# An AdaLN feed-forward kernel with low-rank adapters and a mixture of experts: which queue carries which load, and in which order

## The chip, the cores and the metric

The kernel runs on one core of a Trainium2 chip. The time is device microseconds (us) of one execution. The kernel before takes 495.52 us, the median of three runs (491.48 to 496.64).

Engines are named as in the profile: PE does matrix products (PEld its weight loads), DVE and ACT do elementwise work, POOL is GpSimd, SP only issues transfers. A transfer can be issued from SP (queue q1), ACT (q10) or POOL (q0).

## What is computed

All data is float32. `x` is 8 batches of 512 tokens by 2048 features. Each batch picks, by its token `itok`, one of 8 adapters of rank 16, and the adapter's output `c` goes through a linear layer with a routed low-rank update:

```
c    = (x @ B_sel.T) @ A_sel.T                       # rank 16: conditioning's B and A
base = c @ base_w.T + base_b                         # 2048 x 2048
res  = c @ ffn_A.T                                   # 64 wide
p    = softmax(c @ router_w.T)                       # 16 experts; the top two, renormalized
out  = x + base + 0.5 * sum_e comb[e] * (res @ ffn_B[e].T)
```

Since `c` has rank 16, the kernel never forms it. It multiplies the eight selected `A` (8 x 16 = 128 columns) with `base_w` once into a small matrix `G`, folds `ffn_A` and the router into tables in the same way, and then handles each batch's tokens with short contractions.

## The kernel before

**Two parts.** The first part prepares the weights: it loads and transposes `base_w`, forms `G`, and transposes the experts `ffn_B`. It runs from the start to about 157 us. The main loop then takes the 8 batches, each in 16 tiles of 128 tokens by 512 outputs.

**The first part's backbone** is 128 products, n = 0 to 127 (`w_product`, line 792). `base_w` comes in 8 pieces of 2.10 MB, 16 products to a piece. A piece is loaded as four transfers of 512 KB, one for each quadrant q of 32 partitions, in packets of 2 KB (`load_w`, line 272). There are four buffers, so piece n waits for the transposes of piece n - 4 (`s_wt`). DVE transposes 32 x 32 blocks for each product (`w_transpose`), at most 8 products ahead of PE. Product 0 also needs the selected columns of conditioning's `A` (`take_a`, after DVE's seventh transpose), 1.05 MB that lie in HBM in runs of 128 bytes: 32 transfers of 32 KB, 8192 packets in all (`load_cond_a`).

**Between the products** PE's order is fixed by hand. `E_AT` maps a product number to an expert group: ahead of products 12, 20, 30, 38, 50, 58, 66, 74, 97, 104, 111 and 119, PE transposes ("flips") the groups 0 to 11. Groups 12 to 15 follow at tiles 0, 1, 2 and 5 of the main loop (`E_LATE`). A group is 0.52 MB over all 128 partitions, in packets of 1 KB. It goes into one of four slots (`E_SLOT`); its load waits until the slot's last group is flipped (`s_ef`), and is issued by ACT in `copy_experts`, behind that flip. PE waits in `expert_flips` for the group's load. The products 80 to 95 have batch 0's `x` transposed beside them (`X_AT`), from `xquad0`, 4.19 MB loaded by `load_x0`.

**Who issues what.** SP: quadrants 0 and 1 (partitions 0 to 63) of all `base_w` pieces and of `xquad0`, half of conditioning's `A`, the bias, then the stores of `G`, its reloads (`load_gm`), and loads of `x` for the main loop. POOL: quadrants 2 and 3 (partitions 64 to 127) of the `base_w` pieces and of `xquad0`, between its own computing. ACT: the other half of conditioning's `A`, all of `B`, `ffn_A` and the router (`load_small`, 0.66 MB), and all experts. Each queue executes its instructions in program order: a wait holds everything behind it on that engine.

Of the kernel before, what the change touches and what calls it, by code (L numbers as in the profile page):

```python
# [35 lines left out]
P = 128  # L36
# [5 lines left out]
def adaln_ffn(nc, x, itok, cond_A, cond_B, base_w, base_b, ffn_A, ffn_B, router_w, out):  # L42
    NB, T, D = x.shape
    NAD, _, RK = cond_A.shape
# [37 lines left out]
    with ExitStack() as ctx:  # L82
# [130 lines left out]
        E_AT = {12: 0, 20: 1, 30: 2, 38: 3, 50: 4, 58: 5, 66: 6, 74: 7, 97: 8, 104: 9, 111: 10, 119: 11}  # L213
        E_LATE = {0: 12, 1: 13, 2: 14, 5: 15}
        E_SLOT = (0, 1, 2, 0, 1, 2, 0, 1, 2, 0, 1, 3, 0, 1, 3, 0)
        E_FIRST, E_FRESH, EIN_AT = 3, 11, 98
        GHI_AT, GLO_AT = 34, 38
        XRES_AT, XQ_AT = 104, 120
        EB = 0
# [10 lines left out]

            return [k for k in range(g + 1, GROUPS) if E_SLOT[k] == E_SLOT[g]][:1]

        def load_experts(eng, g):

            c, q, i = e_where(g)
            if e_users(g):
                eng.wait_ge(s_ef, e_users(g)[-1] + 1)
            elif g == E_FRESH:
                eng.wait_ge(s_bxq, KD)
            eng.dma_start(e_in[E_SLOT[g]], bexp_v[c, q, i]).then_inc(s_ein[E_SLOT[g]], 16)  # L240

        def load_small(eng, qs):

# [28 lines left out]
        def load_w(eng, n, qs):  # L272

            need(eng, s_wt, (n - WB + 1) * KD)
            for q in qs:
                eng.dma_start(w_in[n % WB][q * SQ:(q + 1) * SQ], w_q[n, q]).then_inc(s_load[q // 2][n % WB], 16)
# [10 lines left out]
        def load_cond_a(eng, ns):  # L287

            for n in ns:
                for q in range(NQ):  # L290
                    eng.dma_start(conda_q[q * SQ:(q + 1) * SQ, n, :, :], condA_q[n, q]).then_inc(s_conda, 16)  # L291
# [8 lines left out]
        @block.sync  # L300
        def _(sp):
            def store_g(g):

                sp.wait_ge(s_glo, g + 1)
                sp.dma_start(g_dram[:, :, g * BANK:(g + 1) * BANK].rearrange("l p o -> p l o"),
                             g_out[g]).then_inc(s_gst, 16)

            def load_gm(b, c):

                for rep in range(2):  # L310
                    for l in range(2):
                        row = (2 * rep + l) * RK
                        sp.dma_start(f32(gm_r[row:row + RK, c * BANK:(c + 1) * BANK]),
                                     g_dram[l, b * RK:(b + 1) * RK, c * BANK:(c + 1) * BANK]).then_inc(s_gm[c], 16)

            load_w(sp, 0, (0, 1))
            for row in (64, 96):
                sp.dma_start(bias_n[row:row + 1, :], base_b.rearrange("(a o) -> a o", a=1)).then_inc(s_bias, 16)
            load_cond_a(sp, range(0, NAD // 2))
            for n in range(1, 6):  # L320
                load_w(sp, n, (0, 1))
            load_x0(sp, (0, 1))
            store_g(0)
            load_w(sp, 6, (0, 1))
            load_w(sp, 7, (0, 1))
            store_g(1)
            sp.wait_ge(s_gst, 32)
            for c in range(2):
                load_gm(0, c)
            sp.wait_ge(s_wt, 6 * KD)  # L330
            for c in range(0, OC, 2):
                load_xres(sp, 0, c)
            store_g(2)
            sp.wait_ge(s_wt, 7 * KD)
            load_xquad(sp, 1, 0, (0, 1))
            sp.wait_ge(s_gst, 48)
            load_gm(0, 2)
            sp.wait_ge(s_wt, 8 * KD)
            load_xquad(sp, 1, 1, (0, 1))
            store_g(3)  # L340
            sp.wait_ge(s_gst, 64)
            load_gm(0, 3)

            def step(b, f):
                for c in range(OC):
                    if f is None and c == OC - 1:
                        for t in range(NT):
                            sp.wait_ge(s_out, b.n * MT + NT * c + t + 1)
                            sp.dma_start(out_v[b.n, :, t, c * BANK:(c + 1) * BANK],
                                         xres[:, t, c * BANK:(c + 1) * BANK]).then_inc(s_store[c], 16)  # L350
                        continue
                    if f is not None and c < 2 and not is_last(f):
                        xquad_free(sp, f, c)
                        load_xquad(sp, f.n + 1, c, range(0, NQ // 2))
                    sp.wait_ge(s_out, b.n * MT + NT * (c + 1))
                    sp.dma_start(out_v[b.n, :, :, c * BANK:(c + 1) * BANK],
                                 xres[:, :, c * BANK:(c + 1) * BANK]).then_inc(s_store[c], 16)
                    if f is None:
                        continue
                    load_gm(f.n, c)  # L360
                    if c > 0:
                        reload(b, f, c - 1)
                if f is not None:
                    reload(b, f, OC - 1)

            def reload(b, f, c):

                sp.wait_ge(s_store[c], b.n * 16 + 16)
                load_xres(sp, f.n, c)

            batches(step)
            for c in range(OC):
                sp.wait_ge(s_store[c], 16 * NB + (16 * (NT - 1) if c == OC - 1 else 0))
# [1 line left out]

        @block.gpsimd
        def _(pool):
            load_w(pool, 0, (2, 3))
            pool.memset(ffna_q[:, R // SQ, :], 0.0).then_inc(s_const, 1)
            pool.wait_ge(s_const, 1)  # L380
            pool.memset(ident[:, :], 0.0).then_inc(s_idn, 1)
# [1 line left out]
            pool.affine_select(out=ident[:, :], in_=ident[:, :], compare_op=ALU.not_equal, fill=1.0, base=0,  # L383
                               pattern=[[-1, P]], channel_multiplier=1).then_inc(s_idn, 1)

            load_w(pool, 1, (2, 3))
            fills = [(f32(gm_r[64:P, :]), 0.0), (table[:, :, :], 0.0), (f32(sbx_r[64:P, :, :]), 1.0)]
            pool.wait_ge(s_idn, 2)
            for n, (where, value) in enumerate(fills):
# [4 lines left out]
            pool.wait_ge(s_iota, 1)  # L394
            pool.wait_ge(s_tok, 16)
            ids = [adapter(pool, b) for b in range(NB)]
            load_w(pool, 2, (2, 3))
            load_w(pool, 3, (2, 3))

            pool.wait_ge(s_bias, 32)  # L400
            for n, row in enumerate((64, 96)):
# [2 lines left out]
            pool.tensor_tensor(gm_r[96:97, :], bias_n[96:97, :], f32(gm_r[96:97, :]), ALU.subtract)\  # L404
                .then_inc(s_biaslo, 1)

            load_w(pool, 4, (2, 3))
            pool.wait_ge(s_bT, KC)
            pool.wait_ge(s_biaslo, 1)
            for b in range(NB):  # L410
                pool.tensor_copy(bT[:, :, b // 2, b % 2 * RK:(b % 2 + 1) * RK],
                                 bT_all[:, :, bass.ds(ids[b], 1), :].rearrange("p j n k -> p j (n k)"))\
                    .then_inc(s_bsel, 1)
            load_w(pool, 5, (2, 3))
            load_x0(pool, (2, 3))
            for n in range(6, PIECES):
                load_w(pool, n, (2, 3))

            def front(f):

# [26 lines left out]
        def _(act):  # L447
# [2 lines left out]

            act.dma_start(tok[:, :], itok.rearrange("(a b) -> a b", a=1)).then_inc(s_tok, 16)
            load_cond_a(act, range(NAD // 2, NAD))
            load_cond_b(act, range(NQ))
            act.wait_ge(s_const, 1)
            load_experts(act, 0)
            load_small(act, range(NQ))
            for g in range(1, E_FIRST):
                load_experts(act, g)
            act.wait_ge(s_idn, 2)
            act.activation(mx[:, 0:1], ident[:, 0:1], ACT.Copy)  # L460

            def copy_experts(g):

                act.wait_ge(s_ef, g + 1)
                for k in e_next(g):
                    load_experts(act, k)
                for at, there, count in ((0, s_a, NB), (0, s_bT, KC), (1, s_fat, 2), (1, s_sm, 1),
                                         (2, s_xe, KD)):
                    if g == PER_C * at:
                        act.wait_ge(there, count)  # L470
                c, q, i = e_where(g)
                src = ps[:, EB:EB + 2, :].rearrange("p b o -> p (b o)")\
                    .rearrange("p (a h m) -> p a m h", a=EG, h=2)
                dst = bexpT[q * R:(q + 1) * R, c, i * EG:(i + 1) * EG, :].rearrange("r a (m h l) -> r l a m h", h=2, l=2)
                for l in range(2):
                    ins = copy(dst[:, l], src[l * R:(l + 1) * R])
                ins.then_inc(s_ec, 1)
# [49 lines left out]

            first = Batch(0)
            for n in range(NW):
                if n == EIN_AT:  # L530
                    load_experts(act, E_FRESH)
                if n == XRES_AT:
                    act.wait_ge(s_wt, 6 * KD)
                    for c in range(1, OC, 2):
                        load_xres(act, 0, c)
                if n == XQ_AT:
                    act.wait_ge(s_wt, 7 * KD)
                    load_xquad(act, 1, 0, (2, 3))
                if n == NW - 1:
                    act.wait_ge(s_wt, NW)  # L540
                    load_xquad(act, 1, 1, (2, 3))
                if n >= GHI_AT and n % (2 * KD) == GHI_AT % (2 * KD):
                    g_hi(n // (2 * KD) - 1)
                if n in E_AT:
                    copy_experts(E_AT[n])
                if n in SLOT_AT:
                    if SLOT_AT[n] in UP_AT:
                        act.wait_ge(s_gst, 16 * (W_GROUPS - 1))
                    slot(first, SLOT_AT[n], False)
# [235 lines left out]
        def _(pe):  # L785
# [16 lines left out]

            def expert_flips(g):

                pe.wait_ge(s_ein[E_SLOT[g]], 16 * (len(e_users(g)) + 1))
                need(pe, s_ec, g)
                for k in range(2 * EG):
                    ins = flip(EB + k // 4, k % 4 * P, e_in[E_SLOT[g]][:, k // 2, k % 2 * P:(k % 2 + 1) * P])
                ins.then_inc(s_ef, 1)
# [134 lines left out]
```

## Time and profile before

| | |
|---|---|
| median of three runs | 495.52 us (491.48 to 496.64) |
| the profiled execution | 494.57 us, of which the span is 492.4 us |
| PE busy | 415.0 us (84%) |
| DVE busy | 292.1 us (59%) |
| ACT busy, POOL busy | 109.1 us (22%), 58.7 us (12%) |
| moved by DMA | 135.30 MB, mean 275 GB/s |
| DMA queues: share of 16 engines' span | q1 (SP) 60.4%, q10 (ACT) 20.0%, q0 (POOL) 8.2% |
| chain that ended last | PE 64%, DVE 12%, DMA 11%, ACTq 7% |

The span runs from the first to the last instruction of the profiled execution; 2.2 us lie around it. Queue names with a q at the end (ACTq) are an engine's issuing of transfers. The chain is the work that ended last, followed back step by step to what released it.

### The profile page before, as it was taken

Reading aid. Unit: us, or ns where it says so; the run is one execution under the profiler, and the core shown is the slowest. Engines: PE = TensorE matmul, PEld = TensorE weight load, DVE = VectorE, ACT = ScalarE, POOL = GpSimd, SP = SyncE. Lnnn points to the kernel's source line nnn. Section 1 sums busy time; section 2 is a strip of 40 time slices with the busy share of each in tenths; the row PEclk is TensorE's granted clock in tenths of the full one; section 3 lists DMA queues with packets and bytes.
Section 4 is the critical chain, followed back from the end, with each engine's and each line's share of the span. In section 5 each row is a group of like instructions: output and inputs, shape, how many; then the busy total and the mean of one; then the engine's idle time right before and its main releaser. Section 6 shows DMA issues by size and latency. Waiting matters only on the chain.

```text
span 492.4 us, 6151 instructions
## 1 busy us (share of the span) xinstructions
PE 415.0 (84%) x2240; PEld 276.2 (56%) x2240; DVE 292.1 (59%) x699; ACT 109.1 (22%) x166; POOL 58.7 (12%) x72
## 2 busy tenths in 40 slices
PE   0009199577898899999999999999999999999997
PEld 0008178463574556656655665665566566556675
DVE  0116266448682665675766667566776755776453
ACT  0001150330362623202311320230121023013210
POOL 5800210100011001200300120120012012001200
PEclk9999699979998999999999999999999999999999
DMA  8999999996799589988978998897999899835854
GB/s 187 216 251 243 278 273 291 298 281 192 254 279 303 168 269 325 324 285 288 375 274 289 342 322 283 294 366 269 293 354 323 274 289 366 300 121 177 309 194 172
DMA packets 95059, 135.30 MB, mean 275 GB/s; under 512 B 13812, under 2 KB 50676, under 8 KB 95028
## 3 DMA queue, kind: packets, MB, share of 16 engines
q1 hardware_dynamic: 62516, 97.03, 60.4%
q10 hardware_dynamic: 29666, 27.40, 20.0%
q0 software_dynamic: 2848, 10.49, 8.2%
q8 instruction: 18, 0.29, 0.3%
q14 instruction: 11, 0.09, 0.1%
HBM read 99.24 MB, written 35.65 MB: 274 GB/s over the span
## 4 chain that ended last, share of the span: by engine, by line
PE 64%; DVE 12%; DMA 11%; ACTq 7%; ACT 3%; issue 2%; DVEq 0%
PE ps L835 12%; PE ps L852 12%; DMA early_u<-in_L_ffn_B 11%; PE ps L853 10%; PE ps L854 10%; PE ps L865 6%; DVE xT L670 5%; PE ps L855 5%; ACTq L291 5%; PE ps L790 4%; PE ps L800 3%; DVE h_r L651 3%; ACT bexpT L449 2%; DVE early L611 2%; DVE xbuf L778 2%
## 5 line engine op out<-in xcount | busy, mean ns | idle before, releaser
L778 DVE TENSOR_TENSOR xbuf<-ps,xbuf 128x512 f32<-128x512 f32 x128 | 87.2, 681 | 108.1 <-PE ps L855 107.9
L852 PE MATMUL ps<-h_r,u_r 128*128 128x512 f32 x256 | 109.6, 428 | 7.1 <-DVE xbuf L778 7.1
L800 PE MATMUL ps<-early 128*128 128x256 f32 x256 | 65.1, 404 | 43.9 <-DVE early L589 36.8
L853 PE MATMUL ps<-h_r,u_r 128*128 128x512 f32 x256 | 100.4, 392 | 0.0
L854 PE MATMUL ps<-h_r,u_r 128*128 128x512 f32 x256 | 100.1, 391 | 0.0
L800 PEld LDWEIGHTS ps<-early 128*128 128x128 f32 x256 | 49.6, 202 | 56.2 <-issue 37.0
L852 PEld LDWEIGHTS ps<-h_r,u_r 128*128 128x128 f32 x256 | 48.1, 188 | 48.6 <-issue 20.9
L670 DVE STREAM_TRANSPOSE xT<-xbuf 128x512 f32<-128x512 f32 x112 | 72.3, 685 | 0.3 <-PE ps L790 0.3
L835 PE MATMUL ps<-bexpT,cur 128*32 128x512 f32 x512 | 62.9, 609 | 2.1 <-DVE h_r L651 2.1
L611 DVE STREAM_TRANSPOSE early<-xbuf 128x256 f32<-128x256 f32 x128 | 48.2, 421 | 26.3 <-PE ps L800 17.1
L449 ACT ACTIVATE h_r<-ps 128x512 fp32r<-128x512 f32 x64 | 35.7, 594 | 88.3 <-issue 55.9
L854 PEld LDWEIGHTS ps<-h_r,u_r 128*128 128x128 f32 x256 | 48.1, 188 | 11.0
L853 PEld LDWEIGHTS ps<-h_r,u_r 128*128 128x128 f32 x256 | 48.3, 189 | 9.5 <-issue 1.7
L449 ACT ACTIVATE bexpT<-ps 64x1024 f32<-64x1024 f32 x32 | 35.2, 1100 | 75.4 <-PE ps L790 62.1
L855 PE MATMUL ps<-gm_r,sbx_r 128*128 128x512 f32 x128 | 50.0, 391 | 0.0
L651 DVE TENSOR_TENSOR h_r<-ps,h_r 128x512 fp32r<-128x512 f32 x64 | 40.6, 676 | 4.6 <-ACT h_r L449 4.6
L427 POOL TENSOR_TENSOR sbx_r<-bx,sbx_r 32x512 fp32r<-32x512 f32 x8 | 10.3, 1285 | 264.9 <-ACT sbx_r L449 264.9
L865 PE MATMUL ps<-xT,bT 128*32 128x512 f32 x256 | 35.2, 594 | 0.0
L790 PE MATMUL ps<-ident,early_u 128*128 128x128 f32 x112 | 16.6, 296 | 18.5 <-DMA early_u<-in_L_ffn_B 17.1
L835 PEld LDWEIGHTS ps<-bexpT,cur 128*32 128x32 f32 x512 | 13.5, 109 | 32.8 <-issue 30.0
L434 POOL TENSOR_TENSOR u_r<-tmp,u_r 128x512 fp32r<-128x512 f32 x16 | 20.6, 1289 | 70.9 <-ACT u_r L449 70.3
L855 PEld LDWEIGHTS ps<-gm_r,sbx_r 128*128 128x128 f32 x128 | 24.0, 188 | 5.3
(66 smaller groups left out, 218.3 us busy)
## 6 DMA issues: line engine op xcount, KB each, us to landing
out<-xbuf SPq DMA_DIRECT2D x31, 1024.0 KB, 6.9
xbuf<-in_x SPq DMA_DIRECT2D x30, 1024.0 KB, 6.8
xbuf<-in_x SPq DMA_DIRECT2D x28, 512.0 KB, 8.3
xbuf<-in_x ACTq DMA_DIRECT2D x28, 512.0 KB, 9.4
xbuf<-in_L_ffn_base_w SPq DMA_DIRECT2D x16, 512.0 KB, 17.7
xbuf<-in_L_ffn_base_w POOLq DMA_DIRECT2D x16, 512.0 KB, 12.0
early_u<-in_L_ffn_B ACTq DMA_DIRECT2D x14, 512.0 KB, 16.5
gm_r<-g_hilo SPq DMA_DIRECT2D x128, 32.0 KB, 6.1
```

The source lines that it names most:

```text
L449: return act.activation(dst, src, ACT.Copy)
L611: dve.transpose(wT[:, n % RING, :].rearrange("p (t l) -> p t l", l=SQ), src).then_inc(s_wt, 1)
L651: dve.tensor_tensor(h_r[:, c % 2, 1, h, :], ps[:, HB + h, :], f32(h_r[:, c % 2, 0, h, :]), ALU.subtract).then_inc(s_hlo, 1)
L670: dve.transpose(xT[:, j % XRING, :].rearrange("p (t l) -> p t l", l=SQ), src).then_inc(s_xe, 1)
L778: dve.tensor_tensor(xs, ps[:, ACC + t % 2, :], xs, ALU.add).then_inc(s_out, 1)
L800: pe.matmul(ps[:, ACC + g // 2 % 2, g % 2 * WN:(g % 2 + 1) * WN], a_t[:, s, :], wT[:, n % RING, :], start=(s == 0), stop=(s == KD - 1)).th ...
L835: ins = pe.matmul(ps[32 * j:32 * j + 32, HB + h, :], cur[:, b.q, 0:2 * RK], bexpT[:, c, 4 * h + j, :], start=True, stop=True)
L852: pe.matmul(acc, u_r[:, b.q, 0, h, tok_t], hi, start=(h == 0), stop=False)
L853: pe.matmul(acc, u_r[:, b.q, 0, h, tok_t], lo, start=False, stop=False)
L854: pe.matmul(acc, u_r[:, b.q, 1, h, tok_t], hi, start=False, stop=False)
L855: pe.matmul(acc, sbx_r[:, b.q, tok_t], gm_r[:, c * BANK:(c + 1) * BANK], start=False, stop=True)\
L865: pe.matmul(ps[at:at + BK, BXB, :], bT[:, j, f.half, :], xT[:, j % XRING, :], start=(j < NQ), stop=(j >= KD - NQ)).then_inc(s_bxq, 1)
```

## The change

Loads are dealt out again. SP and ACT each issue the same list of loads in the same order: SP the quadrants 0 and 1, ACT the quadrants 2 and 3. The expert groups, so far whole transfers from ACT, become two transfers of 64 partitions, one from each engine, and the flip waits for both (32 instead of 16). POOL issues no transfer any more. The conditioning's `A` is moved ahead of the first `base_w` piece; its two halves stay with SP and ACT. On ACT the late pieces are issued from points of its own loop (`PIECE_AT`, `X0_AT`), and on SP the experts stand between the pieces and the stores.

```diff
-        E_FIRST, E_FRESH, EIN_AT = 3, 11, 98
+        E_FRESH, EIN_AT = 11, 98
+        PIECE_AT, X0_AT = {10: 4, 26: 5, 42: 6, 58: 7}, 26
...
-        def load_experts(eng, g):
+        def load_experts(eng, g, h):
...
-            eng.dma_start(e_in[E_SLOT[g]], bexp_v[c, q, i]).then_inc(s_ein[E_SLOT[g]], 16)
+            half = slice(h * (P // 2), (h + 1) * (P // 2))
+            eng.dma_start(e_in[E_SLOT[g]][half], bexp_v[c, q, i, half]).then_inc(s_ein[E_SLOT[g]], 16)
...
-            load_w(sp, 0, (0, 1))
+            load_cond_a(sp, range(0, NAD // 2))
             for row in (64, 96):
                 sp.dma_start(bias_n[row:row + 1, :], base_b.rearrange("(a o) -> a o", a=1)).then_inc(s_bias, 16)
-            load_cond_a(sp, range(0, NAD // 2))
-            for n in range(1, 6):
-                load_w(sp, n, (0, 1))
+            load_w(sp, 0, (0, 1))
+            load_w(sp, 1, (0, 1))
+            load_cond_b(sp, (0, 1))
+            load_w(sp, 2, (0, 1))
+            load_experts(sp, 0, 0)
+            sp.wait_ge(s_const, 1)
+            load_small(sp, (0, 1))
+            load_w(sp, 3, (0, 1))
+            load_experts(sp, 1, 0)
+            load_experts(sp, 2, 0)
+            load_w(sp, 4, (0, 1))
+            load_experts(sp, 3, 0)
+            load_experts(sp, 4, 0)
+            load_w(sp, 5, (0, 1))
             load_x0(sp, (0, 1))
+            load_experts(sp, 5, 0)
+            load_experts(sp, 6, 0)
             store_g(0)
             load_w(sp, 6, (0, 1))
+            load_experts(sp, 7, 0)
             load_w(sp, 7, (0, 1))
+            load_experts(sp, 8, 0)
+            load_experts(sp, 9, 0)
             store_g(1)
+            load_experts(sp, 10, 0)
             sp.wait_ge(s_gst, 32)
             for c in range(2):
                 load_gm(0, c)
             sp.wait_ge(s_wt, 6 * KD)
             for c in range(0, OC, 2):
                 load_xres(sp, 0, c)
+            load_experts(sp, 11, 0)
             store_g(2)
+            load_experts(sp, 12, 0)
             sp.wait_ge(s_wt, 7 * KD)
             load_xquad(sp, 1, 0, (0, 1))
             sp.wait_ge(s_gst, 48)
             load_gm(0, 2)
+            load_experts(sp, 13, 0)
+            load_experts(sp, 14, 0)
             sp.wait_ge(s_wt, 8 * KD)
             load_xquad(sp, 1, 1, (0, 1))
             store_g(3)
             sp.wait_ge(s_gst, 64)
             load_gm(0, 3)
+            load_experts(sp, 15, 0)
...
# on POOL: every load_w(pool, ...) and load_x0(pool, (2, 3)) is taken out
...
             load_cond_a(act, range(NAD // 2, NAD))
-            load_cond_b(act, range(NQ))
+            load_w(act, 0, (2, 3))
+            load_w(act, 1, (2, 3))
+            load_cond_b(act, (2, 3))
+            load_w(act, 2, (2, 3))
+            load_experts(act, 0, 1)
             act.wait_ge(s_const, 1)
-            load_experts(act, 0)
-            load_small(act, range(NQ))
-            for g in range(1, E_FIRST):
-                load_experts(act, g)
+            load_small(act, (2, 3))
+            load_w(act, 3, (2, 3))
+            load_experts(act, 1, 1)
+            load_experts(act, 2, 1)
...
                 for k in e_next(g):
-                    load_experts(act, k)
+                    load_experts(act, k, 1)
...
             for n in range(NW):
+                if n in PIECE_AT:
+                    load_w(act, PIECE_AT[n], (2, 3))
+                if n == X0_AT:
+                    load_x0(act, (2, 3))
                 if n == EIN_AT:
-                    load_experts(act, E_FRESH)
+                    load_experts(act, E_FRESH, 1)
...
-                pe.wait_ge(s_ein[E_SLOT[g]], 16 * (len(e_users(g)) + 1))
+                pe.wait_ge(s_ein[E_SLOT[g]], 32 * (len(e_users(g)) + 1))
```

## Rows read from the trace of the kernel before

**Rows 1.** Page, 40 slices of the span (12.3 us each): busy tenths, clock, rate.
```profile
PE   0009199577898899999999999999999999999997
...
PEclk9999699979998999999999999999999999999999
DMA  8999999996799589988978998897999899835854
```

**Rows 2.** Timeline of PE: start, us, engine, line, operation, tiles, count [idle before].
```profile
36.82 8.07 PE L800 MATMUL ps<-early 128*128 128x256 f32 x24 [36.82 <-DVE early L589]
44.73 1.04 PE L790 MATMUL ps<-ident,early_u 128*128 128x128 f32 x8
...
59.61 1.97 PE L790 MATMUL ps<-ident,early_u 128*128 128x128 f32 x8 [10.39 <-DMA early_u<-in_L_ffn_B]
...
66.34 1.04 PE L790 MATMUL ps<-ident,early_u 128*128 128x128 f32 x8
...
70.67 1.04 PE L790 MATMUL ps<-ident,early_u 128*128 128x128 f32 x8
...
84.67 1.04 PE L790 MATMUL ps<-ident,early_u 128*128 128x128 f32 x8
...
89.00 1.04 PE L790 MATMUL ps<-ident,early_u 128*128 128x128 f32 x8
...
100.18 1.97 PE L790 MATMUL ps<-ident,early_u 128*128 128x128 f32 x8 [6.69 <-DMA early_u<-in_L_ffn_B]
```

**Rows 3.** Timeline of DVE: the first transposes and the selection of `A`.
```profile
13.78 2.40 DVE L611 STREAM_TRANSPOSE early<-xbuf 128x256 f32<-128x256 f32 x7 [8.92 <-DMA xbuf<-in_L_ffn_base_w]
...
34.85 1.71 DVE L589 COPY early<-bexpT 128x256 f32 x8 [18.67 <-DMA bexpT<-in_L_cond_A]
```

**Rows 4.** Chain that ended last, its pieces in time: start, us, what.
```profile
34.10 25.46 DMA early_u<-in_L_ffn_B
...
71.80 28.34 DMA early_u<-in_L_ffn_B
```

**Rows 5.** Timeline of the two issuing queues, SP and ACT.
```profile
2.34 22.73 SPq L291 DMA_DIRECT2D bexpT<-in_L_cond_A  x16
...
1.31 22.99 ACTq L291 DMA_DIRECT2D bexpT<-in_L_cond_A  x16
...
29.73 0.46 ACTq L240 DMA_DIRECT2D early_u<-in_L_ffn_B  x1
...
34.10 3.23 ACTq L240 DMA_DIRECT2D early_u<-in_L_ffn_B  x2
```

**Rows 6.** Stretches: from:to us, busy by engine, clock, DMA share, GB/s last.
```profile
35.00:37.00 2.00, 0.18 (x1) 0.21 (x2) 1.92 (x9) 0.00 (x0) 0.00 (x0) 1.00 1.06 357
...
67.00:71.00 4.00, 4.00 (x24) 3.54 (x23) 0.72 (x2) 2.77 (x3) 0.14 (x1) 1.00 1.05 218
75.00:85.00 10.00, 9.36 (x68) 8.22 (x66) 5.95 (x18) 0.00 (x0) 1.16 (x2) 1.00 1.05 292
105.50:113.50 8.00, 7.42 (x36) 5.90 (x36) 8.00 (x21) 3.85 (x4) 0.00 (x0) 1.00 1.08 255
118.00:125.00 7.00, 4.36 (x24) 2.08 (x16) 6.87 (x15) 0.00 (x0) 0.00 (x0) 1.00 0.17 41
178.00:179.50 1.50, 1.50 (x8) 1.23 (x7) 1.50 (x4) 1.49 (x2) 0.00 (x0) 1.00 1.00 335
```

**Rows 7.** Queues, 67 to 71 us: packets, MB, share of 16 engines.
```profile
q1 hardware_dynamic: 356, 0.70, 85.8%
q0 software_dynamic: 39, 0.16, 16.8%
```

**Rows 8.** Queues, 178 to 179.5 us.
```profile
q10 hardware_dynamic: 235, 0.24, 48.5%
q1 hardware_dynamic: 236, 0.25, 47.5%
```

**Rows 9.** All DMA, 17 to 18 us.
```profile
DMA packets 1382, 0.18 MB, mean 177 GB/s; under 512 B 1379, under 2 KB 1379, under 8 KB 1382
```

**Rows 10.** Loads of experts (line 240) in the whole trace, issue to landing.
```profile
DMA to landing us min/median/max: 6.3/13.8/29.9
```

**Rows 11.** Around group 15: ACT's issue, SP's reload ahead, PE's flip.
```profile
160.72 0.39 ACTq L240 DMA_DIRECT2D early_u<-in_L_ffn_B  x1
...
164.41 1.71 SPq L313 DMA_DIRECT2D gm_r<-g_hilo  x4
...
176.59 0.87 PE ps L790 x8
```

More of the change, by code:

```diff
@@ L377, in _ @@
         def _(pool):
-            load_w(pool, 0, (2, 3))
             pool.memset(ffna_q[:, R // SQ, :], 0.0).then_inc(s_const, 1)
@@ L384, in _ @@
                                pattern=[[-1, P]], channel_multiplier=1).then_inc(s_idn, 1)
-            load_w(pool, 1, (2, 3))
             fills = [(f32(gm_r[64:P, :]), 0.0), (table[:, :, :], 0.0), (f32(sbx_r[64:P, :, :]), 1.0)]
@@ L396, in _ @@
             ids = [adapter(pool, b) for b in range(NB)]
-            load_w(pool, 2, (2, 3))
-            load_w(pool, 3, (2, 3))
             pool.wait_ge(s_bias, 32)
@@ L405, in _ @@
                 .then_inc(s_biaslo, 1)
-            load_w(pool, 4, (2, 3))
             pool.wait_ge(s_bT, KC)
@@ L413, in _ @@
                     .then_inc(s_bsel, 1)
[L414 to L417, printed above, removed]
             def front(f):
```

## The prediction

> **What bounds the kernel now.** I read the page's slices first. PE is at 8 or 9 tenths from slice 10 on; what it lacks lies in the first ten, while the DMA digits stand at 9 up to 111 us [rows 1]. So the main loop is bound by PE and its partners, and the part ahead of it by transfers. The timeline of PE then says where it waits. It starts at 36.82 us; ahead of group 1 it stands 10.39 us, ahead of group 6 6.69 us, both times for an expert load [rows 2]. The start waits for conditioning's `A`: DVE had its first seven transposes done by 16 us and then stood 18.67 us for `A` [rows 3]. The chain of waits agrees: its two long pieces are loads of experts, 25.46 and 28.34 us from issue to landing, for 0.52 MB each [rows 4]. They are long because the queues share the engines with `base_w` and `xquad0`, much of which nobody needs yet.
>
> After group 6's flip at 100.18 us no load ends a wait of PE; from 118 us the DMA share falls to 0.17 [rows 6], and the stretch is set by DVE and PE. The edit keeps that work as it is. So I count from flip to flip up to group 6, and shift the other 392 us with it.
>
> **The profiled execution** took 494.57 us (span 492.4), 0.95 us under the median of 495.52; the sum is made against 494.6 and I leave the difference alone.
>
> **How fast loads run.** This decides the case, and the stretches differ widely [rows 6]:
> - 67 to 71 us, nearly all SP's lower 64 partitions (q1 0.70 of 0.87 MB [rows 7]): 218 GB/s.
> - 105.5 to 113.5 us, SP's lower-half `base_w` beside ACT's whole experts: 255.
> - 75 to 85 us, SP, POOL and ACT together: 292.
> - 178 to 179.5 us, the main loop's `xquad`, SP lower and ACT upper half, 236 and 235 packets of 1 KB [rows 8]: 335.
> - 35 to 37 us, SP's `base_w` in the lower half beside the last quadrants of conditioning's `B` from ACT, which are the upper half, 2 KB packets: 357.
>
> One half alone is slow, the two halves side by side are fast, and uneven mixes lie between. The edit makes every load from `base_w` piece 0 on look like the last two. I take 340 GB/s, nearer to the 335 that a whole matched load showed; the ends are 292 (what three queues did) and 370 (a little over the 357 row).
>
> **Part by part.**
> *Conditioning's `A` first.* 8192 packets of 128 bytes; with only these in the queues 1382 go in a microsecond [rows 9], 5.9 us. Issuing 16 per queue at 0.46 us each (an issue that was not held up [rows 5]) gives 7.4 us; before, it took 22.7 and 23.0 us, with `base_w` in the way. From 1.3 us, plus some 3 us to land, I take 12 us. Upper end: as slow as before, 24 us, 12 us more.
>
> *Loads from there,* in MB behind `A`: `base_w` piece 0 2.10; piece 1 4.19; `B` 5.24; piece 2 7.34; group 0 7.86; small 8.52; piece 3 10.62; group 1 11.14; group 2 11.67; piece 4 13.76; groups 3 and 4 14.81; piece 5 16.91; `xquad0` 21.10; group 5 21.63; group 6 22.15. Landing = 12 + MB / 0.340 + 1 us: piece 0 at 19.2, group 0 at 36.1, group 1 at 45.8, group 5 at 76.6, group 6 at 78.1.
>
> *PE from there.* First product: 19.2 + 2.40 (seven transposes) + 1.97 (34.85 to 36.82) [rows 2, 3] = 23.6, against 36.8. Product 12's flip would be due 7.9 us on, at 31.5, and waits for group 0 until 36.1; group 1 makes it wait from 40.4 (a flip and eight products take 4.33, as from 66.34 to 70.67) to 45.8. Then the steps of before hold: group 1 to 2 6.73 us (59.61 to 66.34), to 3 4.33, to 4 14.00, to 5 4.33 [rows 2], so group 5's flip is due at 75.2. It now lies behind `xquad0` in both queues and lands at 76.6: a wait of 1.4. Group 6's flip: 76.6 + 4.33 = 80.9 against 100.18, **19.3 us earlier**. The flip after a stall took 1.97 and not 1.04 us [rows 2]; it comes without one now, 0.9 us more. Sum so far 494.6 - 20.2 = 474.4.
>
> *Issues moved to ACT.* ACT gets 16 piece transfers and two of `xquad0` at about 0.46 us, half of them within its loop. It is 22% busy and its copies follow flips that have slack, so I cost the issuing at nothing. Not so a full queue: two issues took 3.23 us instead of 0.9 at 34 us [rows 5]. At product 26 ACT puts piece 5 and 2.1 MB of `xquad0` into its queue, and group 2's copy waits behind them on ACT, and PE's next flip for that copy. Between 0 and 2.3 us for each such crowd; I add 1.6 in all.
>
> *Issues taken off POOL.* Its own early work (bias, selection of `B`) is needed at product 80, far behind; nothing on the path. *Experts in halves:* 16 more issues of about 0.4 us on SP, which does nothing else: nothing, except where SP's order holds one back (the fourth case below). *SP's waits:* the flip waits that now stand in SP's order hold back the pieces behind them. Piece 6 stands behind groups 5 and 6 (flips 2 and 3, at 52 and 57 us), and is needed at product 96, after 105 us: covered. If the store of the first `G` slice comes late behind `xquad0`, ACT's copy of the second slice waits at product 66: the slice is ready at about 57 us, the queue is through at about 79, the need is at 81. That cover is thin, and part of the 1.6.
>
> Forecast: **476 us**. With 370 GB/s group 5 lands at 71.5 and no longer counts; group 1 at 43.1 plus 33.7 gives 76.8 for group 6: 472 with the 1.6. With 292, group 5 lands at 87.1 and group 6 flips at 91.4: 487. With no load late at all after the first product, the steps of before give 69.7, or 463.
>
> **Rivals.**
> *Rate stays as it was* (255 to 292 GB/s). For it: the same 16 engines at share 1.00 to 1.08 in every one of these stretches [rows 6], so they looked full already; three queues become two. Against it: 335 and 357 on two queues. At 275, group 5 lands at 91.7, group 6 flips at 96.0: 4.2 + 0.9 gained, 491 with the 1.6; over the band 487 to 498.
>
> *The halves don't add, slower.* Place: PE's wait for group 5, which used to have ACT's queue nearly to itself and now stands behind 4.19 MB of `xquad0` on both queues. If a half beside the other half ran no faster in sum than the 218 of a half alone, group 5 lands at 13 + 21.63 / 0.218 = 112.2 and group 6 flips at 116.5 instead of 100.2: 494.6 + 16.3 = 511. It decides below 21.63 / (100.2 - 4.3 - 13) = 261 GB/s. For it: 218 and 255 are this low [rows 6]. Against: both come from stretches in which the upper half had little or nothing to move. The Trainium skill, "SBUF — State Buffer", section "Can I just issue two DMAs to hit both halves?", says that two transfers at once, one at partition 0 and one at partition 64, ran only 6% faster than one. By it the stream would do 1.06 x 218 = 231 GB/s, group 6 would flip at 111, and the kernel would take some 505 us; the 335 of the matched `xquad` speaks against it, in a row that holds exactly that pattern.
>
> *Late halves.* Group 15's lower half is issued by SP behind the reload that ends at 166.1 us, where ACT issued the whole at 160.72; PE flips it at 176.59 [rows 11]. By the median landing of 13.8 us it comes at 179.9, 3.3 us late; by the shortest, 6.3, not at all [rows 10]. With two full-queue stalls on ACT of 2.3 on top: 474.4 + 7.9 = 482.
>
> **Chances.** Forecast as it stands (470 to 480) 0.64; rate as before 0.14, of which 0.09 is still faster by over 1% and 0.05 within 1%; halves don't add 0.07, of which 0.06 slower; late halves or a slow start with `A` 0.15, all faster. One per cent, about 5 us, is what a measurement of this kernel tells from no change: faster is under 490.6. That makes faster 0.88, same 0.06, slower 0.06. The range takes in 463 to 472 in part and the slow ends of the cases up to the 491: 466 to 490; what is left out is most of the slow cases and a full 463.
>
> **What would show it.** Right: between 15 and 75 us a rate near 340, queues q1 and q10 with equal packets; PE starting at 23 to 25 us, waits ahead of groups 0 and 1 of about 5 us each, a short one ahead of group 5, group 6 flipped at 79 to 84, and from there to the end 391 to 394 us. Wrong: a rate of 290 or less there; PE's start after 30 us; ACT's issues at product 26 drawn out over 3 us with a flip waiting for ACT; a wait for group 15 in the main loop; or a main loop that has lost what the first part gained.

## The result, and the profile after

The kernel after takes 476.21 us, the median of 4 runs (475.00 to 478.50), against 494.75 us for the kernel before: ratio 0.964, 95% interval 0.957 to 0.971. In all that follows, three executions far above the rest of their kernel (519.93 us of one, 500.14 and 1447.30 us of another) are left out of medians and ratios. The profiled execution took 477.38 us, with a span of 475.1, 17.3 us less than before.

The slices of the page, which answer to [rows 1] (11.9 us each now):

```profile
PE   0066979978888999999999999999999999999996
...
PEclk9997888999999999999999999999999999999999
DMA  7999999937998889799989988998897899754844
```

Slices are counted from 0. PE starts in slice 2 instead of 3, and the transfers have done their work by the end of slice 7 (95 us) instead of slice 8 (111 us). The main loop looks the same. The clock digits stand at 7 and 8 in four slices running, 3 to 6; before, single slices (4, 8, 12) were low.

PE's timeline, the first products and the eight flips that answer to [rows 2]:

```profile
23.80 7.90 PE L823 MATMUL ps<-early 128*128 128x256 f32 x24 [23.80 <-DVE early L612]
36.98 1.97 PE L813 MATMUL ps<-ident,early_u 128*128 128x128 f32 x8 [5.28 <-DMA early_u<-in_L_ffn_B]
...
48.19 1.06 PE L813 MATMUL ps<-ident,early_u 128*128 128x128 f32 x8 [3.98 <-ACT bexpT L464]
...
55.10 1.04 PE L813 MATMUL ps<-ident,early_u 128*128 128x128 f32 x8
...
62.91 1.91 PE L813 MATMUL ps<-ident,early_u 128*128 128x128 f32 x8 [3.32 <-ACT bexpT L464]
...
78.00 1.91 PE L813 MATMUL ps<-ident,early_u 128*128 128x128 f32 x8
...
83.33 1.04 PE L813 MATMUL ps<-ident,early_u 128*128 128x128 f32 x8
...
87.65 1.04 PE L813 MATMUL ps<-ident,early_u 128*128 128x128 f32 x8
```

The waits of 10.39 and 6.69 us for loads are gone. Of PE's waits ahead of flips, one for a load is left, ahead of group 0, and two for ACT's copies have come up, ahead of groups 1 and 3. The forecast's short wait for group 5's load did not come, since flip 5 itself came late. Group 6 is flipped at 87.65 instead of 100.18 us.

DVE's rows that answer to [rows 3], and the landing of conditioning's `A` (line 293; issue to landing):

```profile
19.55 2.40 DVE L634 STREAM_TRANSPOSE early<-xbuf 128x256 f32<-128x256 f32 x7 [15.48 <-DMA xbuf<-in_L_ffn_base_w]
21.87 1.67 DVE L612 COPY early<-bexpT 128x256 f32 x8
```

```profile
DMA to landing us min/median/max: 1.8/2.1/2.5
```

Stretches of the first part, with the granted clock, the DMA share and GB/s last:

```profile
6.00:10.00 4.00, 0.00 (x0) 0.00 (x0) 0.00 (x0) 0.00 (x0) 0.00 (x0) 1.00 0.84 129
...
14.00:20.00 6.00, 0.00 (x0) 0.00 (x0) 0.45 (x2) 0.00 (x0) 5.38 (x2) 1.00 1.06 316
20.00:30.00 10.00, 6.20 (x17) 5.11 (x18) 6.97 (x22) 0.00 (x0) 0.00 (x0) 1.00 1.06 355
30.00:50.00 20.00, 10.74 (x43) 8.80 (x43) 7.70 (x19) 3.66 (x4) 2.80 (x8) 0.81 1.07 336
50.00:60.00 10.00, 9.59 (x42) 7.86 (x41) 4.70 (x11) 2.17 (x2) 0.00 (x0) 0.86 1.08 314
60.00:70.00 10.00, 7.09 (x38) 6.27 (x39) 5.05 (x11) 4.94 (x5) 0.00 (x0) 0.83 1.05 374
```

The same view over 14 to 76 us, the stretch that the forecast priced at 340 GB/s, and the queues from 60 to 65 us (packets, MB, share):

```profile
14.00:76.00 62.00, 38.97 (x172) 32.46 (x172) 29.17 (x73) 10.76 (x11) 8.19 (x10) 0.89 1.07 342
```

```profile
q1 hardware_dynamic: 471, 0.93, 52.7%
q10 hardware_dynamic: 475, 0.94, 52.6%
```

342 GB/s over the stretch, with nearly equal packets in both queues. The share of the 16 engines is no higher than before (1.07, against 1.05 to 1.08 in the busy stretches of [rows 6]); the same share simply moves more bytes.

Last, ACT's timeline around its two late copies:

```profile
45.87 2.18 ACT L464 ACTIVATE bexpT<-ps 64x1024 f32<-64x1024 f32 x2 [12.00 <-DVE xT L640]
...
56.23 4.36 ACTq L242 DMA_DIRECT2D early_u<-in_L_ffn_B  x1
60.63 2.13 ACT L464 ACTIVATE bexpT<-ps 64x1024 f32<-64x1024 f32 x2 [8.46 <-issue]
```

The copy of group 0 waited for DVE's transposes of `B`. The copy of group 2 waited behind the loads that ACT issues there; the last of them, of group 5, took 4.36 us to issue.

### The profile page after: what moved, and what is told of

Same layout as the page of the kernel before. It is cut to its first block, busy times and chain, and to the rows that moved or that the text cites. A ratio compares the mean times of both kernels' runs of the same rounds, so it can differ in the third digit from the quotient of the medians.

```text
span 475.1 us, 6167 instructions
## 1 busy us (share of the span) xinstructions
PE 417.1 (88%) x2240; PEld 279.3 (59%) x2240; DVE 293.7 (62%) x699; ACT 109.0 (23%) x166; POOL 47.9 (10%) x54
## 4 chain that ended last, share of the span: by engine, by line
PE 68%; DVE 14%; ACTq 5%; ACT 5%; DMA 4%; issue 3%; DVEq 0%
PE ps L858 12%; PE ps L875 12%; PE ps L876 10%; PE ps L877 10%; PE ps L888 7%; DVE xT L693 5%; PE ps L878 5%; PE ps L823 5%; PE ps L813 4%; DMA early_u<-in_L_ffn_B 4%; ACT bexpT L464 4%; DVE h_r L674 3%; DVE early L634 2%; DVE xbuf L801 2%; ACTq L293 2%
## 5 line engine op out<-in xcount | busy, mean ns | idle before, releaser
L823 PE MATMUL ps<-early 128*128 128x256 f32 x256 | 67.8, 418 | 28.1 <-DVE early L612 23.8
L823 PEld LDWEIGHTS ps<-early 128*128 128x128 f32 x256 | 52.2, 212 | 40.3 <-issue 24.0
L858 PE MATMUL ps<-bexpT,cur 128*32 128x512 f32 x512 | 61.6, 598 | 2.3 <-DVE h_r L674 2.3
L813 PE MATMUL ps<-ident,early_u 128*128 128x128 f32 x112 | 17.3, 306 | 14.5 <-ACT bexpT L464 9.2
```

Of the source, the lines that this page charges most:

```text
L823: pe.matmul(ps[:, ACC + g // 2 % 2, g % 2 * WN:(g % 2 + 1) * WN], a_t[:, s, :], wT[:, n % RING, :], start=(s == 0), stop=(s == KD - 1)).th ...
L858: ins = pe.matmul(ps[32 * j:32 * j + 32, HB + h, :], cur[:, b.q, 0:2 * RK], bexpT[:, c, 4 * h + j, :], start=True, stop=True)
```

## The experiments

Ratios are to the kernel before, run beside each kernel, with 95% intervals.

**Is it the pairing of halves?** Only the quadrants are dealt out otherwise, for every quadrant load of the first part:

```diff
-            load_w(sp, 0, (0, 1))
+            load_w(sp, 0, (0, 2))
...
-            load_w(act, 0, (2, 3))
+            load_w(act, 0, (1, 3))
```

> The kernel after with the quadrants dealt out otherwise: SP issues 0 and 2, ACT 1 and 3, of base_w, B, ffn_A, the router and batch 0's xquad0; queues, order, sizes and packets stay, and the experts stay in lower and upper halves. So both queues now write the lower 64 partitions at once, then both the upper. Theory (it is the pairing of a lower with an upper half that makes loads fast): the stretches of 2 KB packets fall from the 360 to 375 GB/s of the kernel after to 220 to 250, group 5 lands 15 us or more later, and the kernel takes 488 to 500. Rival (two matched queues in one order are enough, whatever partitions they write): rate and time as in the kernel after, 476 to 478.

Measured 509.70 us, ratio 1.031 (1.028 to 1.035): some 33 us slower than the kernel after, beyond the theory's band of 488 to 500; the rival is out. Its stretches, and its queues from 80 to 90 us, when both move piece 5 or `xquad0`:

```profile
14.00:80.00 66.00, 24.43 (x100) 20.56 (x100) 19.75 (x51) 5.85 (x6) 8.16 (x10) 0.81 1.08 236
```

```profile
DMA packets 1083, 2.15 MB, mean 215 GB/s; under 512 B 34, under 2 KB 34, under 8 KB 1083
...
q1 hardware_dynamic: 543, 1.08, 53.5%
q10 hardware_dynamic: 540, 1.07, 53.3%
```

Two matched queues, 2 KB packets, both in the same half: 215 GB/s, about the 218 of a nearly lone queue [rows 6, 7]. The kernel after moves the same transfers in the same order and packets from 60 to 70 us, in opposite halves, at 374. The time is worse than the slower stream alone would make it, because the full queue now holds ACT: group 5's load took it 9.22 us to issue, and flip 3 waited 11.20 us. One thing stays open. A quadrant is also a quarter of each row in HBM, so the exchange changes which addresses are read side by side too; no run keeps those and changes the partitions alone.

**What is it worth that POOL issues none?** The upper quadrants of `base_w` and `xquad0` are given back to POOL, in its old places:

```diff
-            load_w(act, 0, (2, 3))
...
+            load_w(pool, 0, (2, 3))
             pool.memset(ffna_q[:, R // SQ, :], 0.0).then_inc(s_const, 1)
```

> The kernel after with the upper quadrants of base_w and of batch 0's xquad0 issued by POOL where it issued them before; experts, B, ffn_A and router in halves from SP and ACT, A first, all else as after. It tells what taking the loads off POOL is worth. Theory: POOL's packets of about 4 KB against SP's 2 KB make its half finish first and leave SP's alone, conditioning's A is slowed beside it, and the rate falls to about 290 GB/s; ACT's full queue at product 26 is gone, which is worth 3 us. Together 482 to 488. Rival (only order and halves count): 473 to 477, as the kernel after or better by ACT's stall.

Measured 499.76 us, ratio 1.012 (1.007 to 1.016), 12 us above the theory's band. SP and POOL still load opposite halves, yet the gain is gone: opposite halves are needed, and they are not enough. Its first transposes, and 14 to 80 us:

```profile
34.16 2.40 DVE L636 STREAM_TRANSPOSE early<-xbuf 128x256 f32<-128x256 f32 x7 [29.31 <-DMA xbuf<-in_L_ffn_base_w]
```

```profile
14.00:80.00 66.00, 32.42 (x157) 27.62 (x158) 26.27 (x65) 10.81 (x11) 16.99 (x21) 0.95 1.09 254
```

15 us are lost before the first product: SP's part of piece 0 stands behind `A`, and `A` crawls beside POOL's packets. From 5 to 30 us POOL's queue moved 3.81 MB in 1058 packets, 3.6 KB each, and the transfers of `A` landed after 9.3 us in the median, where the kernel after needed 2.1. From 14 to 80 us the rate is 254, where the kernel after has 344, and flip 5 waits 13.98 us for its load. How much of this is the size of POOL's packets and how much its places in the order, no run tells apart.

**`A` first, alone, in the kernel before:**

```diff
-            load_w(sp, 0, (0, 1))
+            load_cond_a(sp, range(0, NAD // 2))
             for row in (64, 96):
...
-            load_cond_a(sp, range(0, NAD // 2))
-            for n in range(1, 6):
+            for n in range(0, 6):
```

> The kernel before with one part of the change alone: SP issues its half of conditioning's A ahead of base_w's piece 0 (ACT always did). Theory (the loads bind in sum): PE starts earlier, near 30 us instead of 36.8, but waits longer ahead of group 1, whose load still lands near 59 us behind the same bytes; 493 to 495, no gain. Rival (the start is what counts): the 6 us stay, 488 to 489.

Measured 498.81 us, ratio 1.010 (1.006 to 1.015): slower, which neither theory said. DVE's first transposes come at 34.46 us, as in the run above, instead of 13.78, and PE starts at 39.18 instead of 36.82, not near 30.

**`A` not first, in the kernel after:**

```diff
-            load_cond_a(sp, range(0, NAD // 2))
+            load_w(sp, 0, (0, 1))
             for row in (64, 96):
...
-            load_w(sp, 0, (0, 1))
+            load_cond_a(sp, range(0, NAD // 2))
# and the same exchange on ACT
```

> The kernel after with one part of the change undone: on both queues base_w's piece 0 goes ahead of conditioning's A. In the kernel after, A alone moved only 129 GB/s from 6 to 10 us, its 32 KB transfers being issued one per 0.5 us, and each landed in 2.1 us: the engines ran short of work. Theory (issue-bound): with piece 0 in the queue first, its 2.1 MB go while A is being issued; A and piece 0 are both in by 15 to 17 us instead of 19.5, PE starts at 18 to 20 us instead of 23.8, group 0 lands 4 to 5 us earlier, and the kernel takes 472 to 474. Rival (A first is what made the start early): PE starts at 26 us or later, 478 to 482.

Measured 483.23 us, ratio 0.975 (0.968 to 0.981). My theory (472 to 474) fell, and the rival came nearer in the time (478 to 482) and not in the start (26 us or later): PE did start a little earlier, at 23.06 us, but group 0 came at 40.40 instead of 36.98 and group 6 at 93.48 instead of 87.65. Its stretches, and its queues from 14 to 22 us and from 50 to 60 us:

```profile
6.00:14.00 8.00, 0.00 (x0) 0.00 (x0) 1.48 (x5) 0.00 (x0) 3.57 (x2) 1.00 1.23 234
14.00:22.00 8.00, 0.00 (x0) 0.00 (x0) 1.83 (x8) 0.00 (x0) 4.70 (x2) 1.00 1.20 198
```

```profile
q1 hardware_dynamic: 2216, 1.24, 86.2%
q10 hardware_dynamic: 2153, 0.34, 33.4%
...
q10 hardware_dynamic: 1194, 1.67, 71.0%
q1 hardware_dynamic: 782, 0.98, 38.7%
```

Mixing `A` with large packets did cost something: up to 30 us this kernel moved a mean of 233 GB/s and the kernel after 247, some 0.4 MB or 1.2 us apart. But that is the smaller part. The queues also moved unequal bytes, 1.24 against 0.34 MB from 14 to 22 us and 0.98 against 1.67 from 50 to 60, long after `A`, when the rate was 265 where the kernel after had 314; so halves stood unpaired again. Most of group 6's 5.8 us arises after 30 us; which of the two causes it is not shown. In time, `A` first is worth 4 to 6 us in the kernel after (the gain over the kernel before is 16.5 and 18.5 us with it, 12.4 without) and costs 4 in the kernel before. The two kernels differ in more than POOL; that POOL's loads turn the sign is likely from the run above, whose first transposes came as late, and not shown by itself.

**Whole experts from ACT, the rest as after:**

```diff
-            half = slice(h * (P // 2), (h + 1) * (P // 2))
-            eng.dma_start(e_in[E_SLOT[g]][half], bexp_v[c, q, i, half]).then_inc(s_ein[E_SLOT[g]], 16)
+            eng.dma_start(e_in[E_SLOT[g]], bexp_v[c, q, i]).then_inc(s_ein[E_SLOT[g]], 16)
...
-            load_experts(sp, 0, 0)
# and so on: SP issues no experts
```

> The kernel after with one part undone: the expert groups are whole transfers of 128 partitions, all issued by ACT at the same places; SP issues none; base_w, B, ffn_A, router and xquad0 stay in halves on the two queues. Theory (unequal queues fall out of step): SP runs ahead, so halves of base_w meet 1 KB packets of experts (255 GB/s in the kernel before) and not each other; ACT's queue ends later, group 5 lands near 90 us, and the kernel takes 484 to 490. Rival (only base_w and xquad0 need pairing; experts are a quarter of the bytes): 476 to 480.

Measured 481.43 us, ratio 0.971 (0.964 to 0.978), between the two bands. From 14 to 80 us it moves 321 GB/s, where the kernel after has 344. The queues fell out of step as the theory said: from 50 to 60 us ACT's moved 2.48 MB and SP's 0.04, 252 GB/s in all. Group 0 is flipped at 41.17 and group 6 at 91.91, 4.2 and 4.3 us later than in the kernel after. The time is 2 to 4 us longer by the gains over the kernel before, but the intervals overlap, so from the times alone it is not told from nothing.

**The hidden stall of the kernel before.** SP stores the first slice of `G` ahead of its half of `xquad0`:

```diff
-            load_x0(sp, (0, 1))
             store_g(0)
+            load_x0(sp, (0, 1))
```

> The kernel before with two lines of SP's order exchanged: the store of the first slice of G ahead of SP's half of xquad0. Theory (a hidden stall of the kernel before): that store was issued at 71.44 us behind 2.1 MB of xquad0 and landed 32.8 us later, at 104.2, and ACT's copy of the second slice, and DVE behind it, waited for it. With the store first it lands by 85, the copy is done by 95, and the stretch from group 6's flip to group 8's takes 24 us instead of 28: 490 to 491. Rival (the profile names PE as the releaser of that copy, and PE is what it waited for): the copy stays behind group 6's flip, and the time at 494 to 496.

Measured 494.38 us, ratio 1.001 (0.998 to 1.004). In the kernel before, ACT's copy of the second slice came here, and the stores landed so (line 305):

```profile
104.29 0.60 ACT L449 ACTIVATE u_r<-ps 128x512 fp32r<-128x512 f32 x1 [11.53 <-PE ps L800]
```

```profile
DMA to landing us min/median/max: 4.0/11.4/32.8
```

The first store was issued at 71.44; 32.8 us later it is 104.2. With the store ahead, the copy runs at 93.99, so the store was what it waited for, although the profile names PE. But nothing is gained: group 7's flip then waits 2.42 us for its load and DVE 1.91 us for `xquad0`, and from flip 6 to flip 8 it is 28.07 us again. The stall was real and covered another. In its profiled execution flips 6 and 8 came 2.0 us earlier all the same, and that was lost again by flip 12, at 159.90 against 159.60; the last section shows where.

**The two waits on ACT's copies.** Three kernels and the kernel after once more, side by side:

```diff
-        AT_AT, BT_AT, FA_AT, GA_AT, SEL_AT = 6, 24, 40, 46, 54
+        AT_AT, BT_AT, FA_AT, GA_AT, SEL_AT = 6, 16, 40, 46, 54
...
-        PIECE_AT, X0_AT = {10: 4, 26: 5, 42: 6, 58: 7}, 26
+        PIECE_AT, X0_AT = {10: 4, 26: 5, 42: 6, 58: 7}, 32
```

> One number is changed in the kernel after: ACT issues its half of xquad0 at product 32, behind the copy of group 2, instead of at product 26, ahead of it. Theory (a full queue holds ACT): there, issuing group 5's load took ACT 4.36 us, the copy ended 7.8 us after flip 2, and flip 3 waited 3.32 us for it. With xquad0 behind, the issue takes under 1 us, flip 3 follows flip 2 by 4.4 us instead of 7.8, and 3.3 us are gained: about 473 where the kernel after has 476. Rival (the loads bind anyway): groups 5 and 6 or the store of the first slice come no earlier, a later flip waits for a load, and the time stays within 1 us of the kernel after.

> One number is changed in the kernel after: DVE transposes conditioning's B after its transpose 16 instead of 24, while PE stands ahead of group 0. Theory: in the kernel after the copy of group 0 waits 12.0 us for these transposes (they come after product 16), and flip 1 waits 3.98 us for the copy. Moved ahead, flip 1 comes at 44 to 46 us instead of 48.2. But the queues then are as full as before when ACT issues group 5, so most of it is given back in ACT's stall at product 26: 475.5, 0 to 1 us faster than the kernel after. Rival (the two waits are independent): the whole 2.5 to 3.5 us stays, 473.

> The two edits together: B's transposes after transpose 16, ACT's xquad0 at product 32. Theory: neither wait on ACT's copies is left; flip 1 at 44 to 46 us, flip 3 by 57, and flip 5 waits for group 5's load behind xquad0, as the prediction had it. Group 6's flip at 81 to 83 us instead of 87.65: 470 to 472. Rival (loads bind): 474 or more.

> The kernel after, unchanged, beside the three variants on the same chip: 476, ratio to the kernel before 0.962 to 0.966. All theories expect the same.

| | median, us | ratio (95% interval) | flip 1 | flip 3 | flip 6 |
|---|---|---|---|---|---|
| kernel after, again | 478.22 | 0.966 (0.963 to 0.969) | 48.36 | 63.86 | 87.68 |
| ACT's `xquad0` at product 32 (`x0_late`) | 475.79 | 0.961 (0.958 to 0.964) | 48.47 | 59.71 | 85.89 |
| `B` transposed after DVE's transpose 16 (`bt_early`) | 477.45 | 0.965 (0.962 to 0.968) | 46.16 | 62.22 | 85.84 |
| both | 475.15 | 0.960 (0.956 to 0.965) | 45.91 | 55.49 | 80.65 |

The flips up to 3 moved as the theories said: `xquad0` late takes flip 3 to 4.33 us behind flip 2; `B` early gains 2.2 us at flip 1, of which flip 3 keeps 1.6, since ACT's stall at product 26 has grown to 5.68 us; both together bring flip 6 to 80.65. The times did not all follow. `xquad0` late gains 4.1 us at flip 3 and only 1.8 at flip 6: from 76 to 82 us PE's granted clock was 0.69, and flip 4 to flip 5 took 6.70 us instead of 4.33. Its time is 2.4 us shorter (its runs, 474.69 to 476.72, lie just below all of the kernel after, 476.77 to 479.93), not the 3.3 expected; `B` early alone is not told from nothing. With both, the time fell in the rival's band (474 or more) and not in the theory's 470 to 472. Of the 7.0 us at flip 6, 4.2 are left at flip 8 (107.52 against 111.67); the medians differ by 3.1, and the six runs with both reach from 472.34 to 478.76. The loss between flips 6 and 8 is in the timeline of PE with both edits:

```profile
76.27 1.09 PE L813 MATMUL ps<-ident,early_u 128*128 128x128 f32 x8 [0.46 <-DMA early_u<-in_L_ffn_B]
...
80.65 1.04 PE L813 MATMUL ps<-ident,early_u 128*128 128x128 f32 x8
...
88.01 1.09 PE L813 MATMUL ps<-ident,early_u 128*128 128x128 f32 x8 [2.86 <-DMA early_u<-in_L_ffn_B]
```

Group 5 waits for its load, as the forecast had it, and group 7 waits 2.86 us behind piece 6.

**Two steps further.** On top of both edits, first group 7 ahead of piece 6 (on ACT piece 6 therefore at product 52, piece 7 at 60), and ACT's last `xquad` issue behind the closing copies:

```diff
-            load_w(sp, 6, (0, 1))
             load_experts(sp, 7, 0)
+            load_w(sp, 6, (0, 1))
...
-        PIECE_AT, X0_AT = {10: 4, 26: 5, 42: 6, 58: 7}, 26
+        PIECE_AT, X0_AT = {10: 4, 26: 5, 52: 6, 60: 7}, 32
...
             h_hi(first, 0)
+            load_xquad(act, 1, 1, (2, 3))
```

> The two edits of x0_late and bt_early, and two more: group 7's load goes ahead of base_w's piece 6 on both queues (in that pair group 7's flip waited 2.86 us for its load behind piece 6), and ACT issues its last xquad half behind the copies that end the first part, where its issue took 3.25 us ahead of them. Theory: 2.9 us from group 7 and 1 to 2.5 us from the end of the first part, against the 475.2 of the two edits: 470 to 472. Rival (the loads bind in sum, piece 6 is late instead): 474 to 476, with DVE waiting for base_w at product 96.

Measured 473.28 us (four runs), ratio 0.954 (0.947 to 0.960). Group 7's wait is gone. It is above the theory's 470 to 472 and just under the rival's 474 to 476; against both edits alone (0.960, 0.956 to 0.965) the intervals overlap, so the gain is not told from nothing.

Then the loads in the order of need:

```diff
             load_w(sp, 0, (0, 1))
+            load_experts(sp, 0, 0)
             load_w(sp, 1, (0, 1))
             load_cond_b(sp, (0, 1))
+            load_experts(sp, 1, 0)
             load_w(sp, 2, (0, 1))
-            load_experts(sp, 0, 0)
+            load_experts(sp, 2, 0)
...
-            load_x0(sp, (0, 1))
             load_experts(sp, 5, 0)
             load_experts(sp, 6, 0)
+            load_x0(sp, (0, 1))
# ACT in the same order; its loads of experts behind the copies
```

> The kernel of the run tuned, with its loads in the order of their need: group 0 behind base_w's piece 0, group 1 behind B, group 2 behind piece 2, groups 5 and 6 ahead of xquad0; ACT issues a group's load behind the copy and not ahead of it, piece 4 at product 14, xquad0 at product 40. Theory (in tuned, PE's waits of 4.3 and 3.3 us ahead of groups 0 and 1 are a matter of order, not of bytes): group 0 lands 8 us earlier, flip 0 comes at 33, flip 1 at 37 to 38, flip 6 at 71 to 76 instead of 85.1, and the kernel takes 464 to 468 where tuned takes 474. Rival (the queues are full of bytes, and ACT with them): the piece transfers hold ACT's copies again, waits for base_w or xquad0 take the place of those for groups, and the time stays at 471 to 475.

Measured 470.37 us, between the theory's band and the rival's 471 to 475; ratio 0.954 (0.949 to 0.958), as the kernel before stood at 494.08 beside it. By the ratio it is not told from the one above. PE's timeline:

```profile
32.40 1.04 PE L811 MATMUL ps<-ident,early_u 128*128 128x128 f32 x8
...
36.75 1.06 PE L811 MATMUL ps<-ident,early_u 128*128 128x128 f32 x8
...
57.24 1.97 PE L811 MATMUL ps<-ident,early_u 128*128 128x128 f32 x8 [10.78 <-DMA early_u<-in_L_ffn_B]
```

Flips 0 and 1 came as expected, with no wait. Then PE stood 10.78 us ahead of group 3: by the forecast's own formula its 14.29 MB land at 12 + 42.0 + 1 = 55.0 us, whatever the order before them. Both queues had the load issued by 41.3 us, and from 14 to 56 us they moved 331 GB/s, so it was not issued too late. So the rival held in kind: the waits moved, and what is left of them is bytes.

## Why the prediction was right

The time was forecast at 476, and it is 476.21 (477.38 in the profiled execution). The mechanism held; that the number agrees so closely is partly luck, since two misses of 5 and 4 us nearly cancel.

| step | forecast | measured |
|---|---|---|
| rate behind `A`, GB/s | 340 | 342 (14 to 76 us) |
| piece 0 in, us | 19.2 | 19.55 |
| first product | 23.6 | 23.80 |
| group 0's flip | 36.1 | 36.98 |
| group 1's flip | 45.8 | 48.19 |
| flip 2 to flip 3 | 4.33 | 7.81 |
| flip 3 to flip 5, with the wait for group 5 | 18.3 + 1.4 | 20.4 + 0 |
| group 6's flip | 80.9 (82.5 with the 1.6) | 87.65 |
| flip 6 to the end of the span | 391.3 | 387.5 |

**The rate** was the step that decided, and it held. I had read it off two short stretches of the kernel before (335 and 357 [rows 6]), and the exchange of quadrants shows that it needs the pairing of opposite halves: 374 against 215 GB/s for the same transfers. The run with POOL shows that pairing alone does not give it, 254 against 344; the two queues that had it moved like packets in step, and those without did not. This also settles the slower rival. It describes a kernel in which the halves are not opposite: such a kernel moved 236 GB/s from 14 to 80 us and took 509.7 us, where 511 had been worked out. That the two agree is partly chance, since 11.20 us of its wait were for ACT and not for a load. The rival does not happen here. The Trainium skill, "SBUF — State Buffer", section "Can I just issue two DMAs to hit both halves?", gives 6% for two transfers at once over one. Here two queues in opposite halves move 374 GB/s and a nearly lone queue in one half 218, 72% more, and the measurement decides.

**`A` first** went as worked out: the last of its transfers was issued at 8.7 us and they landed in 2.1 us, and piece 0 was in at 19.55 against 19.2. I had only half of the reason: with POOL's packets beside it the same transfers took 9.3 us in the median. The part is worth 4 to 6 us here and minus 4 us in the kernel before. My forecast held the parts together without seeing that they may depend on each other.

**"Its copies follow flips that have slack"** is the sentence that failed. Two of ACT's copies had none. Group 0's copy waits for DVE's transposes of `B`, which come after its transpose 24 and so after product 16; I had taken them as hidden in PE's wait, as they were before. It cost 2.4 us at group 1. And at product 26 the full queue held ACT for 4.36 us; I had named the place and the cause, and put 0 to 2.3 us on it, 1.6 in all. It cost 3.5 us at flip 3. Another 2.1 us between flips 3 and 5 are PE's clock: the eight transposes of flips 3 and 4 took 1.91 us instead of 1.04, and from 60 to 80 us the granted clock was 0.83 (0.58 from 76 to 80), where the kernel before had 1.00 from 65 to 85. The forecast had no such term after flip 0. Against these 8 us stands the wait of 1.4 for group 5 that did not come, which leaves flip 6 6.7 us behind the sum. With both copies mended PE's clock was full again in that stretch (flip 4 took 1.04) and flip 6 came at 80.65, against the 80.9 of the sum: the working was sound but for these terms.

**"No load ends a wait of PE after group 6"** was true and too narrow. A store did, through ACT and DVE. In the kernel before, flip 6 to flip 8 took 28.07 us (100.18 to 128.25), in the kernel after 23.99 (87.65 to 111.64): 4.1 us less, of which the forecast had counted only the 0.9 of flip 6's clock. The store now lands within 14.5 us, and the loads that took its place in the exchange on the kernel before no longer end a wait here. So group 6 was 6.7 us later than the sum, of which 1.6 had been allowed for, and the rest of the span 3.8 shorter: 1.3 us in all, the distance from 476.0 to the profiled 477.38.

**The rival "late halves"** did not come: group 15's lower half was issued by SP at 151.74 and flip 15 had no wait for it. "Rate as before" is out with 342.

## What to carry to other kernels

Look at which partitions each queue writes at the same time, not only at how full the DMA engines are: they showed a share of 1.05 to 1.08 at 215, 255 and 374 GB/s alike. When loads get faster, go through every wait that stood in their shadow; here two copies on ACT, one of them behind a full queue, took back some 6 us. A compute engine that issues transfers can be held by them: ACT was, for 4.36 us here and 9.22 in the same-half kernel. Test an edit's parts together as well as alone: "`A` first" had opposite signs in the kernel before and in the kernel after.

## What the runs showed of the hardware that I had not expected

- A queue of 128-byte packets beside one of 2 KB packets leaves the halves unpaired: with conditioning's `A` and `base_w` mixed, the two queues sent nearly equal packets (2216 and 2153 from 14 to 22 us) and so unequal bytes (1.24 and 0.34 MB), at 198 GB/s; with `A` alone first, 129 and then 316 to 355 GB/s. Up to 30 us this cost only some 1.2 us.
- PE's clock after the short wait between the first part and the main loop is not settled by the length of that wait. PE stands ahead of its last 16 products there, the same in every kernel. At full clock they take 1.92 us and at the lower of the two levels, 1.2 instead of 2.4 GHz, up to 3.6. The kernel after, its second profiled run, both edits, and `tuned`:

```profile
138.50 1.92 PE L858 MATMUL ps<-bexpT,cur 128*32 128x512 f32 x16 [2.34 <-DVE h_r L674]
...
139.70 2.58 PE L858 MATMUL ps<-bexpT,cur 128*32 128x512 f32 x16 [3.65 <-DVE h_r L674]
...
134.03 3.62 PE L858 MATMUL ps<-bexpT,cur 128*32 128x512 f32 x16 [2.10 <-DVE h_r L674]
...
135.55 1.92 PE L856 MATMUL ps<-bexpT,cur 128*32 128x512 f32 x16 [2.10 <-DVE h_r L672]
```

After the same 2.10 us the granted clock was 1.00 in one kernel (135.55 to 138 us) and 0.57 in another (134 to 138); the kernel before had 2.10 us too, and 3.24 us for the products. What decides it stays open. It matters when kernels are compared that differ by 2 or 3 us. The group-12 flip behind these products came at 142.08 in the kernel after and at 144.87 in its second profiled run, though the flips of group 8 lay within 0.03 us: of a spread of 2.7 us between the two spans, some 1.6 us are the clock and 1.2 the later start. `store_first` lost its 2.0 us here (3.35 us of waiting and 3.64 us for the products, against 2.10 and 3.24 in the kernel before), and `x0_late` and `bt_early`, level at flips 6 and 8, were 1.4 us apart at flip 12.
